# Causal attention inside a Macaron block: score tiles for the softmax maxima regrouped from one head by 128 queries to four heads by 32 queries

## What is computed

```python
scores = jnp.einsum('bqhe,bkhe->bhqk', q, k) * scale   # 16 heads of 16 features
causal = jnp.tril(jnp.ones((l, l), dtype=bool))
scores = jnp.where(causal[None, None], scores, -jnp.inf)
attn = jax.nn.softmax(scores, axis=-1)
out = jnp.einsum('bhqk,bkhe->bqhe', attn, v)
```

## Time and profile before

| | us |
|---|---|
| runs, median (lowest to highest) | 1339.91 (1338.66 to 1339.95) |
| the profiled execution, its own time | 1341.68 |
| its span, first to last instruction | 1339.6 |
| softmax stage within it, about | 477 to 946 |
| granted TensorE clock, mean over the span | 0.929 of full |

### The profile page before, as it was taken

How to read it: one execution, slowest core, us unless ns; L and a number is a source line. 1 busy time by engine, 2 the same in 40 slices (tenths; PEclk the granted TensorE clock), 3 DMA queues, 4 the chain that set the end, 5 groups by cost and what they waited for, 6 DMA issues and landing times. The chain is left out here.

```text
span 1339.6 us, 38859 instructions
## 1 busy us (share of the span) xinstructions
PE 1163.8 (87%) x13796; PEld 866.7 (65%) x13796; DVE 982.0 (73%) x2151; ACT 793.1 (59%) x1944; POOL 535.3 (40%) x738
## 2 busy tenths in 40 slices
PE   1873999989859969999998999999858659999897
PEld 1653999968748825555554555553746559999686
DVE  6666666648869879998887888893586766666586
ACT  1645666663226606877776777788636466666631
POOL 0642444337715512322332322333516334442576
PEclk9975999989969969999998999999979769999899
DMA  6320444423355651222221222210234114443354
GB/s 206 127 80 28 128 132 134 125 74 95 96 190 196 220 92 47 67 59 62 60 63 52 62 59 60 63 39 3 95 113 128 49 56 131 131 134 111 99 150 137
DMA packets 96384, 132.43 MB, mean 99 GB/s; under 512 B 15644, under 2 KB 81116, under 8 KB 96220
## 3 DMA queue, kind: packets, MB, share of 16 engines
q1 hardware_dynamic: 74716, 86.07, 21.4%
q0 software_dynamic: 13056, 35.67, 9.7%
q10 hardware_dynamic: 8448, 8.39, 1.8%
HBM read 81.35 MB, written 48.23 MB: 97 GB/s over the span
## 5 line engine op out<-in xcount | busy, mean ns | idle before, releaser
L1740 ACT ACTIVATE s_PR<-s_ps_b 128x512 f32<-128x512 f32 (+3 forms) x768 | 331.1, 496 | 123.2 <-PE s_ps_b L1851 118.1
L1760 DVE TENSOR_REDUCE s_MX<-s_ps_a 128x1 f32<-128x512 f32 (+3 forms) x608 | 357.9, 653 | 50.4 <-PE s_ps_a L1829 47.3
L1851 PE MATMUL s_ps_b<-QO,KO 99*32 99x512 bf16 (+3 forms) x3072 | 217.2, 329 | 8.1 <-issue 3.6
L1711 POOL TENSOR_SCALAR_AFFINE_SELECT s_PR<-s_PR 128x256 f32<-128x256 f32 x256 | 103.2, 406 | 301.7 <-ACT s_PR L1740 296.1
L792 POOL DMA_INDIRECT f_XG<-xn_scratch,f_tok_u x144 | 136.1, 945 | 206.2 <-PE f_ps_x L888 137.7
L1829 PE MATMUL s_ps_a<-KO,QO 96*32 96x512 bf16 (+3 forms) x3072 | 212.2, 338 | 1.4 <-DVE s_MX L1760 1.2
L1003 POOL DMA_INDIRECT f_YG<-y_scratch,f_slots_u x128 | 128.3, 1003 | 87.4 <-issue 33.8
L1868 PE MATMUL s_ps_o<-s_PR,s_VG 128*17 128x512 f32 (+3 forms) x1536 | 158.8, 488 | 1.0 <-POOL s_PR L1711 0.6
L898 PE MATMUL f_ps_u<-f_W,f_xh 128*128 x576 | 152.8, 348 | 0.0
L1851 PEld LDWEIGHTS s_ps_b<-QO,KO 99*32 99x32 bf16 x3072 | 81.3, 96 | 90.7 <-ACT s_PR L1740 44.4
L1829 PEld LDWEIGHTS s_ps_a<-KO,QO 96*32 96x32 bf16 x3072 | 81.2, 99 | 69.3 <-DVE s_MX L1760 24.6
(11 more groups left out here) (227 smaller groups left out, 2637.8 us busy)
## 6 DMA issues: line engine op xcount, KB each, us to landing
y_scratch<-f_YS SPq DMA_DIRECT2D x144, 128.0 KB, 1.7
qk_scratch<-p_QK SPq DMA_DIRECT2D x32, 384.0 KB, 3.1
QO<-qk_scratch SPq DMA_DIRECT2D x96, 128.0 KB, 2.8
KO<-qk_scratch SPq DMA_DIRECT2D x96, 128.0 KB, 2.8
xn_scratch<-f_XN ACTq DMA_DIRECT2D x16, 512.0 KB, 4.0
f_RAW<-in_w_up SPq DMA_DIRECT2D x16, 352.0 KB, 3.2
X<-in_x SPq DMA_DIRECT2D x4, 1024.0 KB, 9.4
x_scratch<-X SPq DMA_DIRECT2D x1, 4096.0 KB, 16.4
```

The source lines that it names most:

```text
L1711: nc.gpsimd.affine_select(out=tile, in_=tile, compare_op=ALU.is_ge, fill=0.0, base=0, pattern=[[0, 2], [1, P]], channel_multiplier=-1)\
L1740: nc.scalar.activation(PR[:, u // 2 % SLOTS, u % 2, 0:W - lo], ps_b[u % RING][:, lo:W], ACT.Exp, scale=SCALE).then_inc(exp_done, 1)
L1760: nc.vector.tensor_reduce(MX[:, h:h + heads, i, s], ps_a[slot][:, 0:heads * keys].rearrange("p (h n) -> p h n", h=heads), AX.X, ALU.max).t ...
L1851: last = nc.tensor.matmul(ps_b[u % RING][strip, lo:W], KO[k][0:RM, h, i * P + strip.start:i * P + strip.stop], QO[k][0:RM, h, hf * W + lo: ...
```

## The change

Pass A is cut otherwise. A quad now holds the same 32 queries of four heads, one head in each strip, each strip with its own head's keys moving. There are 40 units (source, half, halves, block m of 32 queries). With source 0 they are the diagonal ones, 32(m+1) keys long, two halves of the queries in one bank for m up to 7; with source 1 they are the second half's queries against the first 512 keys. The mask square is 32 wide in place of 128. MX, NM and what follows take the layout (head and query on partitions, 32 blocks), so that `turn_max` is four float32 products of 32 columns in place of one transpose, and the three transfers read 128 partitions of 64 bytes. The list of units and the tables of places are written anew, with AHEAD = 12; `turn_max` and the first `turn_output` move from place (8, 0) to (8, 3), the second `turn_output` from (4, 3) to (2, 2).

```diff
-    A_UNITS = []
-    for i in range(NQ):
-        for s in range(1 + i // 4):
-            keys = min((i + 1) * P - s * W, W)
-            wide = W // keys
-            A_UNITS += [(i, s, h, min(wide, GH - h), keys) for h in range(0, GH, wide)]
+    Q = P // 4
+    NBLK = W // Q
+    A_UNITS = [(0, 0, 2, 0), (1, 1, 1, 0), (0, 1, 1, 15), (1, 1, 1, 1), (0, 0, 2, 1), (0, 0, 1, 15), (1, 1, 1, 2), (0, 0, 2, 2),
+               (1, 1, 1, 3), (0, 0, 2, 7), (0, 0, 2, 3), (1, 1, 1, 4), (0, 1, 1, 14), (1, 1, 1, 5), (0, 0, 1, 8), (0, 0, 1, 14),
...
+    assert sorted(A_UNITS) == sorted([(0, 0, 2, m) for m in range(NBLK // 2)] +
+                                     [(0, s, 1, m) for s in range(2) for m in range(NBLK // 2, NBLK)] +
+                                     [(1, 1, 1, m) for m in range(NBLK)])
-    A_AFTER = ((0, 2, 0, 1), (1, 2, 0, 1), (2, 0, 0, 1), (0, 1, 1, 0), (1, 1, 0, 1), (1, 0, 1, 3),
-               (1, 2, 1, 0), (0, 0, 4, 0), (0, 0, 1, 0), (1, 2, 0, 0), (0, 0, 2, 2), (0, 0, 2, 0))
-    V_AFTER = ((0, 0, 0, 1), (1, 0, 0, 0), (1, 0, 0, 1), (0, 0, 0, 0), (0, 1, 0, 0), (0, 0, 1, 0),
-               (0, 1, 0, 0), (1, 0, 0, 1), (0, 0, 0, 1), (0, 0, 0, 1), (0, 0, 0, 0), (0, 1, 0, 0))
+    A_AFTER = ((0, 0, 2, 0), (3, 1, 0, 0), (0, 1, 1, 1), (1, 1, 0, 2),
+               (0, 2, 0, 1), (2, 1, 0, 1), (0, 2, 1, 0), (1, 2, 1, 2),
+               (1, 0, 0, 0), (1, 0, 1, 0), (0, 3, 2, 0), (0, 1, 1, 1))
+    V_AFTER = ((0, 0, 0, 1), (1, 0, 0, 1), (0, 0, 0, 0), (1, 0, 0, 0),
+               (0, 1, 0, 0), (1, 0, 1, 0), (0, 0, 1, 0), (0, 0, 0, 0),
+               (1, 0, 0, 0), (0, 0, 0, 1), (0, 0, 1, 0), (0, 1, 0, 0))
-    OUT_0, OUT_1, MAX_AT = (8, 0), (4, 3), (8, 0)
-    COPY_0, COPY_1 = (5, 2), (1, 1)
+    OUT_0, OUT_1, MAX_AT = (8, 3), (2, 2), (8, 3)
+    COPY_0, COPY_1 = (4, 3), (1, 0)
-    AHEAD = NA - 27
+    AHEAD = 12
...
-        NMS = sb("NMS", [GH * NQ, PARTS, P], BF16)
+        NMS = sb("NMS", [P, PARTS, Q], BF16)
...
-                nc.vector.tensor_reduce(MX[:, h:h + heads, i, s],
-                                        ps_a[slot][:, 0:heads * keys].rearrange("p (h n) -> p h n", h=heads),
+                nc.vector.tensor_reduce(MX[:, src, s:s + halves, m],
+                                        ps_a[slot][:, 0:halves * keys].rearrange("p (s n) -> p s n", s=halves),
...
-                nc.vector.tensor_copy(NMT[:, :], ps_a[max_slot(g, k)[1]][0:GH * NQ, 0:P]).then_inc(slot_read, 1)
+                nc.vector.tensor_copy(NMT[:, :], ps_a[max_slot(g, k)[1]][:, 0:Q]).then_inc(slot_read, 1)
...
-                if diagonal:
-                    scores = ps_a[slot][:, 0:heads * keys].rearrange("p (h n) -> p h n", h=heads)
+                if src == 0:
+                    scores = ps_a[slot][:, 0:halves * keys].rearrange("p (s n) -> p s n", s=halves)
                     for strip in STRIPS:
-                        nc.tensor.matmul(scores[strip, :, keys - P:keys], identb[:, strip], neg[:, 0:heads, :],
+                        nc.tensor.matmul(scores[strip, :, keys - Q:keys], identb[:, strip], neg[:, 0:halves, strip],
                                          start=True, stop=False, skip_group_check=True)
-                for h in range(h0, h0 + heads):
-                    at = (h - h0) * keys
-                    for strip in STRIPS:
-                        last = nc.tensor.matmul(ps_a[slot][strip, at:at + keys],
-                                                QO[k][0:R, h, i * P + strip.start:i * P + strip.stop],
-                                                KO[k][0:R, h, s * W:s * W + keys], start=not diagonal,
+                for s in range(s0, s0 + halves):
+                    at = (s - s0) * keys
+                    row = (m + s * NBLK) * Q
+                    first = 0 if src else s * W
+                    for h, strip in enumerate(STRIPS):
+                        last = nc.tensor.matmul(ps_a[slot][strip, at:at + keys], QO[k][0:R, h, row:row + Q],
+                                                KO[k][0:R, h, first:first + keys], start=src == 1,
                                                 stop=True, skip_group_check=True)
...
-                nc.tensor.transpose(ps_a[slot][0:GH * NQ, 0:P], NM[:, :], ident[:, :]).then_inc(maxT_done, 1)
+                for strip in STRIPS:
+                    last = nc.tensor.matmul(ps_a[slot][strip, 0:Q], NM[:, :], ident[:, strip], start=True, stop=True)
+                last.then_inc(maxT_done, 1)
```

More of the change, by code:

```diff
@@ L1599, in softmax_stage @@
         PR = sb("PR", [P, SLOTS, 2, W])
[L1600 to L1603, removed]
-        NMS = sb("NMS", [GH * NQ, PARTS, P], BF16)
+        MX = sb("MX", [P, 2, 2, NBLK])
+        NM = sb("NM", [P, 2 * NBLK])
+        NMT = sb("NMT", [P, Q])
+        NMR = sb("NMR", [P, Q])
+        NMS = sb("NMS", [P, PARTS, Q], BF16)
         OS = sb("OS", [P, W])
@@ L1607, in softmax_stage @@
         identb = sb("identb", [P, P], BF16)
-        zero_b = sb("zero_b", [P, GH, P], BF16)
-        neg = sb("neg", [P, GH, P], BF16)
+        zero_b = sb("zero_b", [P, 2, P], BF16)
+        neg = sb("neg", [P, 2, P], BF16)
         ps_a = [ps(f"ps_a{i}", [P, W]) for i in range(SLOTS_A)]
@@ L1674, in _ @@
             nc.gpsimd.affine_select(out=neg[:, :, :], in_=zero_b[:, :, :], compare_op=ALU.is_ge, fill=NEG, base=0,
-                                    pattern=[[0, GH], [-1, P]], channel_multiplier=1).then_inc(consts, 1)
+                                    pattern=[[0, 2], [-1, P]], channel_multiplier=1).then_inc(consts, 1)
             nc.gpsimd.tensor_copy(identb[:, :], ident[:, :]).then_inc(consts, 1)
@@ L1754, in a_unit @@
             def a_unit(g, k, v):
-                i, s, h, heads, keys = A_UNITS[v]
+                src, s, halves, m = A_UNITS[v]
+                keys = W if src else Q * (m + 1)
                 if v == 0 and since(g, 1):
@@ L1767, in combine @@
                     dve.wait_ge(maxT_done, g)
-                nc.vector.tensor_reduce(NM[:, :].rearrange("p (h i) -> p h i", h=GH), MX[:, :, :, :], AX.X,
+                nc.vector.tensor_reduce(NM[:, :], MX[:, :, :, :].rearrange("p c s m -> p (s m) c"), AX.X,
                                         ALU.max, negate=True).then_inc(max_ready, 1)
@@ L1811, in a_unit @@
             def a_unit(g, k, v):
-                i, s, h0, heads, keys = A_UNITS[v]
-                diagonal = s == i // 4
+                src, s0, halves, m = A_UNITS[v]
+                keys = W if src else Q * (m + 1)
                 q, slot = a_slot(g, k, v)
```

## The result

The changed kernel took 1332.96 us (median of 4 runs, 1330.69 to 1333.13) against 1339.93 for the kernel before in the same comparison: ratio 0.9942, 95% interval 0.9927 to 0.9958. That is 7 us faster, where 23 were forecast; 1332.96 lies above the range of 1306 to 1330. A second comparison on another chip gave 0.9957 (0.9934 to 0.9980).

The account below looks back on a forecast made before the run. PE's stream of columns was taken as the bound; 1.47 us per group times 14.7 gave 21.6, plus DVE's 1.4 and 0.3 before pass B, total 23.3 us, so 1316.6 us, range 1306 to 1330.

Parts of the forecast that it names:

- (f): Path of the maxima from last score quad to next group: slack 0.9 us now, 0.3 to 1.2 after; priced at nothing.
- Rival 3: Maxima late at a group's first pass B quad; 1 us wait loses 15 us (1332); mild shares 0.14, strong 0.03.
- the mild cases: ACT and DVE taking over the bound, or maxima mildly late at pass B: chance together 0.14.
- (a): Pass A score quads: 1536 fewer columns per group, saving 0.64 us, less 0.05 for small quads.
- (b): Mask quads: 1024 columns in 24 quads instead of 4096 in 22, at 0.035 us each, saving 0.96 us per group.
- (g): Tables of places: a tenth of the saving turns into PE waits for ACT's exponentials and DVE's banks.
- the tenth taken off: Share of the per-group PE saving expected to become waits: (1.55 + 0.08) x 0.9 = 1.47 us.
- (c): Different keys in the four strips of a score quad: full pace expected, nothing taken.
- Rival 2: Score quads whose strips have different keys don't run together, taking twice as long: about 1422 us; chance 0.06.
- (d): turn_max as four float32 products: 0.12 us instead of 0.20, saving 0.08.
- (e): DVE's reductions in the first group: 20.3 us instead of 21.75, 1.4 less; in the steady part DVE stays below PE.
- rival 1: ACT and DVE take over the bound; half the saving goes to waits, 1325 to 1332 us; shares chance 0.14.

## Why the prediction was wrong

**The step that failed is (f), the maxima's path.** It added up the path as transposes, normalisation, copy, POOL's split and the third transfer, priced the whole at nothing, and closed with "SP's loads behind these three transfers moved no more than that". It looked at the loads behind the rows and not at the one ahead of them, whose wait for the eighth value step the new table moves by four places. The profile of before shows SP standing nowhere between that load and the rows, because the value step at (8, 3) ended before the rows were ready. What the runs showed in its place: rows issued 1.4 us late, landing 0.9 us later behind the load just issued, 1 us of slack used up, 1.0 to 2.4 us lost in each of 12 groups and 0.6 more at the back edge, 15.5 us more than before in all; taking the order away gave back 20.6 us of the stage, with the clock.

Its slack was misread as well. The 0.9 us came from a third transfer of 2.1 us, but that is the median over the three rows. The range in the kernel before was:

```profile
DMA to landing us min/median/max: 1.8/2.1/3.6
```

In the very group that (f) took its times from, the third row was issued at 694.62 and landed at 697.53, 0.13 us before the next group began. In five other groups it landed after 3.4 to 3.6 us and 0.6 to 0.95 us of stream were lost. So in six of the ten groups whose transfers had a load ahead and whose landing is on the trace, the path had next to no room before anything was moved.

**Rival 3** named the place, the wait of the first pass B quad, but blamed the transfers' size, and got the small part of a chance shared by the mild cases. Its mild form, 1 us a group or 15 us in all, gave 1332; measured were 1333, with 15.5 us more stream lost. That the size fits is luck: the cause it gave costs 0.2 us a transfer.

**The rest of the sum held.** The forecast of 1316.6 us without this wait is what the kernel does with the rows first or the load earlier: 0.9829 and 0.9822 of 1339.9 are 1317 and 1316, which the intervals leave open by some 5 us either way. The distance of the groups is the finer test, and there two errors partly cancelled, as the first point says.

- (a), (b), (g): quads follow the straight line down to 64 columns, 0.03 us; a quad of 32 also takes 0.03, where the line put 0.02. The mask price of 0.035 was a little high. Saving per group forecast 1.47 after the tenth taken off, measured 1.54. By the paces measured, an estimate, the stream of a group shrank by 1.8 us (masks 1.1, score columns 0.6, turn_max 0.1), so that nearer a sixth than a tenth of it went to waits. The Trainium skill's page "TensorEngine Tiling (Array Packing)", Performance Considerations, gives about 60 cycles of overhead for a matmul, the same for one column as for 60. Read per quad, that is an estimate of 0.025 us at 2.4 GHz for anything up to 60 columns, and the 0.029 of the 32-column quads agrees; per instruction it doesn't, since four products share one 0.03.
- (c): strips that move different heads' keys run together, 0.22 us for 512 columns. Rival 2 did not come.
- (d): turn_max fell to 0.08, forecast 0.12.
- (e): the first group's 40 reductions take 20.48 us, as the row below shows; forecast 20.3. From the first reduction to the first pass B quad it is 1.9 us less (25.7 after 27.7), forecast 1.7.

```profile
476.56 20.48 DVE L1767 TENSOR_REDUCE s_MX<-s_ps_a 128x2 f32<-128x64 f32 x40 [0.81 <-PE s_ps_a L1838]
```

- (g) and rival 1: ACT and DVE didn't take over. With the rows first PE is busy for 39.82 of 40 us beside DVE's 35.37.

## What to carry to other kernels

When a change moves a step, follow every semaphore that the step raises to each queue that waits for it, and ask what stands behind that wait, on a DMA queue as on an engine: here one value step paced a load that nobody was in a hurry for, and the transfer behind the load was the one that everybody needed. In the program's order a transfer with a deadline belongs ahead of transfers that are merely paced, or else the paced one has to go out well before it: here 2.3 us were enough and 0.35 were not. A trace shows no wait where slack hides it, so for a path that another step feeds the slack is to be measured before the step is moved, group by group and for the transfer that comes last: a median over three transfers hid that the third was often late.

## What was not expected of the hardware

- A short transfer (8 KB) issued 0.35 us behind a 128 KB load lands after 2.8 to 3.0 us in the median, with the load 1.7 us or more ahead after 2.0. Its being cut into 128 pieces of 64 bytes rather than 32 of 256 costs 0.2.
- The third of three such transfers often lands after 3.4 to 3.8 us where the first two take about 2, in the kernel before (five groups) as in the one with the value step back (eight groups). No run here shows why.
- Quads of 32 and of 64 columns both follow each other at 0.03 us, with four weight loads each: below 64 columns a quad gets no cheaper.
- PE and ACT each stall at their own jump back in a loop, some 4 us and 2.9 us, and straight code for 16 groups showed no stall at all in the stage.
